# Reordering the start-up of a fused attention kernel: two queues, one product, four rows of ones

## The reference, cut to what matters

```
h = layernorm(x + causal_attention(x))            # 16 heads of 16 features
h = layernorm(h + cross_attention(h, context))
h = layernorm(h + relu(h @ w1.T + b1) @ w2.T + b2)
qp = h @ Wq + bq;  kp = ctx @ Wk + bk;  vp = ctx @ Wv + bv      # one head
w  = softmax(qp @ kp.T / 16);  y = w @ vp
g  = sigmoid(concat(qp, y) @ Wg + bg)
out = y * mask * g + h
```

## Time and profile before

| | us |
|---|---|
| three runs | 855.65, 855.28, 859.28 (median 855.65) |
| the profiled execution's own time | 855.65 |
| span of its trace | 853.8 |
| PE busy | 774.1 (91%) |
| DVE busy | 658.6 (77%) |
| POOL busy | 485.9 (57%) |
| ACT busy | 439.7 (52%) |
| start of the second stage (first instructions of SP, PE, POOL) | about 75.6 |

### The profile page before, as it was taken

How to read it: one execution, slowest core, us unless ns; L and a number is a source line. 1 busy time by engine, 2 the same in 40 slices (tenths; PEclk the granted TensorE clock), 3 DMA queues, 4 the chain that set the end, 5 groups by cost and what they waited for, 6 DMA issues and landing times.

```text
span 853.8 us, 19936 instructions
## 1 busy us (share of the span) xinstructions
PE 774.1 (91%) x7214; PEld 643.2 (75%) x7232; DVE 658.6 (77%) x1514; ACT 439.7 (52%) x921; POOL 485.9 (57%) x598
## 2 busy tenths in 40 slices
PE   6997799999999898778789999999999888999886
PEld 4766678888877676556468888888878788889875
DVE  3542768787878888667989999998888776978874
ACT  3532355565665565556555555555544543544542
POOL 1411566776777666554345666566555676657541
PEclk9999999999999999899889999999999999999988
DMA  8486889688767764336332222222200020011222
GB/s 275 137 250 197 160 125 153 130 135 140 128 112 132 120 96 89 79 85 123 76 79 55 54 54 55 53 55 54 54 2 10 2 71 8 29 56 56 83 83 77
DMA packets 105308, 79.63 MB, mean 93 GB/s; under 512 B 43261, under 2 KB 101967, under 8 KB 104947
## 3 DMA queue, kind: packets, MB, share of 16 engines
q1 hardware_dynamic: 101850, 74.17, 41.5%
q10 hardware_dynamic: 3360, 4.18, 1.5%
HBM read 27.03 MB, written 12.97 MB: 47 GB/s over the span
## 4 chain that ended last, share of the span: by engine, by line
PE 62%; DVE 17%; issue 5%; SPq 2%; ACT 2%; DMA 2%; POOL 1%; ACTq 0%; POOLq 0%; DVEq 0%
PE a_misc L88 13%; PE a_pair L88 11%; PE a_s L1009 7%; PE a_pair L796 4%; PE a_s L772 4%; PE a_pair L814 4%; PE a_pair L970 3%; PE a_s L770 3%; PE a_pair L955 3%; PE a_s L932 2%; PE a_pair L1108 2%; PE a_s L88 2%; DVE c_z L1515 1%; PE a_pair L817 1%; SPq L697 1%
## 5 line engine op out<-in xcount | busy, mean ns | idle before, releaser
L1413 DVE TENSOR_REDUCE a_nm<-a_s 128x2 f32<-128x512 f32 (+1 forms) x192 | 127.2, 678 | 56.3 <-PE a_s L772 55.6
L1924 POOL TENSOR_TENSOR c_hidden<-c_hid,c_hidden 128x256 fp32r<-128x256 f32 x128 | 96.0, 750 | 115.2 <-DVE c_hid L1653 114.8
L1174 ACT ACTIVATE a_pT<-a_pair 128x512 f32<-128x512 f32 x192 | 113.7, 597 | 86.4 <-PE a_pair L796 79.1
L1269 ACT ACTIVATE a_pT<-a_pair 77x512 f32<-77x512 f32 x128 | 76.1, 594 | 141.6 <-PE a_pair L955 137.1
L1009 PE MATMUL a_s<-c_w,c_hidden 128*128 128x256 f32 x768 | 117.4, 292 | 0.0
L88 PE MATMUL a_pair<-c_fxh,c_w 128*128 128x256 f32 x512 | 100.7, 289 | 13.9 <-DVE c_hid L1653 13.9
L1831 POOL TENSOR_SCALAR_AFFINE_SELECT a_pT<-a_pT 128x256 f32<-128x256 f32 (+1 forms) x192 | 91.6, 495 | 33.0 <-ACT a_pT L1174 32.6
L1009 PEld LDWEIGHTS a_s<-c_w,c_hidden 128*128 128x128 f32 x768 | 98.9, 190 | 0.4 <-issue 0.4
L88 PEld LDWEIGHTS a_pair<-c_fxh,c_w 128*128 128x128 f32 x512 | 79.2, 191 | 16.8 <-DVE c_hid L1653 16.7
L796 PE MATMUL a_pair<-a_sq,a_sk 98*128 98x256 bf16 (+1 forms) x512 | 76.6, 254 | 7.1 <-ACT a_pT L1174 7.0
L1653 DVE TENSOR_SCALAR c_hid<-a_pair,ff_b_col 128x256 f32<-128x256 f32 x128 | 61.3, 479 | 25.8 <-ACT c_hidden L1295 25.6
(11 more groups left out here) (258 smaller groups left out, 2143.5 us busy)
## 6 DMA issues: line engine op xcount, KB each, us to landing
a_sq<-a_parts SPq DMA_DIRECT2D x96, 128.0 KB, 4.4
a_sk<-a_parts SPq DMA_DIRECT2D x96, 128.0 KB, 4.6
a_sq<-c_parts SPq DMA_DIRECT2D x96, 128.0 KB
x<-in_xT SPq DMA_DIRECT2D x16, 256.0 KB, 6.1
res<-in_x SPq DMA_DIRECT2D x16, 256.0 KB, 5.6
out<-g_fin SPq DMA_DIRECT2D x16, 256.0 KB, 2.1
a_sk<-kc_parts SPq DMA_DIRECT2D x96, 38.5 KB
fold_rows<-x_fold ACTq DMA_DIRECT2D x1, 2496.0 KB, 9.9
```

Source lines behind the costliest of these rows:

```text
L1174: nc.scalar.activation(pT[g % NPT][:], stps[g % 2][:], ACT.Exp).then_inc(s_exp, 1)
L1269: nc.scalar.activation(pT[g % NPX][0:SC], st_ps[0:SC, :], ACT.Exp).then_inc(c_exp, 1)
L1413: nc.vector.tensor_reduce(nm[c % 2][:, QT * heads[0] + qt:QT * heads[-1] + qt + 1:QT], sps[g % 2][:].rearrange("p (h k) -> p h k", h=len(h ...
L1924: nc.gpsimd.tensor_tensor(hl(m), hid[n % NHID][:], f32(hh(m)), ALU.subtract).then_inc(c_hl, 1)
```

## The change

Five things are moved, and nothing that reaches the output changes.

1. The load of WkT goes from SP's queue, where it was first, to ACT's, where it is now first, ahead of WqT and cwk. SP's queue begins with the context.
2. PE's `square(1)` (WvT by wg2) goes from before the key loop to after it.
3. The store of the key parts (`kc_parts`) goes from SP's queue to ACT's, behind the folded keys and `part_one(1)`; on SP, the loads of sequences 2 and 3 go behind the first sequence's stacks.
4. ACT splits sequence 0 one step later in the key loop (after step 4 instead of 3), and POOL makes its low part after all six steps, not after step 4.
5. The three transfers that copied the ones at the start of the second stage are gone, and so is the memset on DVE in the first stage. Instead DVE writes the ones into each of the four stacks by a memset of 2x2048 float32, in slots 8 to 11 of causal position -2, ahead of its first maximum.

```diff
--- before.py
+++ after.py
@@ -37,7 +37,6 @@
 KS = NTERM * DH
 KX = KS + 2
 NSTK, EARLY = 4, 2
-PAIR_OF_ONES = 1.0 + 0x3F80 / 2.0 ** 23
 CB = 6
 CCH = [(c * SC, min(CB, B - c) * SC) for c in range(0, B, CB)]
 SCE = SC + 1
@@ -168,7 +167,6 @@
         @block.sync
         def _(sp):
             src = a["ctxT"].rearrange("(k p) c -> p k c", p=P)
-            sp.dma_start(raw["wkT"], lay(a["WkT"])).then_inc(w_loaded["wkT"], 16)
             for i, (c0, cn) in enumerate(CCH):
                 sp.dma_start(cf[:, :, c0:c0 + cn], src[:, :, c0:c0 + cn]).then_inc(c_loaded[i], 16)
             for n, w in (("cwv", A("ca_wv")), ("wv", a["L1_xattn_Wv"]), ("wg1", a["L1_xattn_Wg"][0:D, :]), ("swq", A("sa_wq")),
@@ -181,17 +179,15 @@
             for n, v in t.cols.items():
                 sp.dma_start(v[:], a[n + "_col"]).then_inc(small, 16)
             sp.dma_start(t.mask[:], a["maskT"]).then_inc(small, 16)
-            sp.wait_ge(s_kp3, KT * NC)
-            sp.dma_start(d.kc.rearrange("p t b x -> p (t b x)"), parts[:].rearrange("p t b k s -> p (t b k s)")).then_inc(k_stored, 16)
             sp.wait_ge(t.s_xl, EARLY)
-            for c in (2, 3):
-                sp.dma_start(t.x[c % 2][:], a["xT"][c].rearrange("(k p) s -> p k s", p=P)).then_inc(t.x_loaded[c % 2], 16)
             sp.wait_ge(t.s_p3, 1)
             for rows, term, i in stack_rows():
                 sp.dma_start(t.first_stack[0][rows].rearrange("r h s -> r (h s)"),
                              t.parts[0][:, 0, term].rearrange("p k s -> p (k s)")).then_inc(t.stacked[0], 16)
                 sp.dma_start(t.first_stack[1][rows].rearrange("r h s -> r (h s)"),
                              t.parts[0][:, 1, i].rearrange("p k s -> p (k s)")).then_inc(t.stacked[0], 16)
+            for c in (2, 3):
+                sp.dma_start(t.x[c % 2][:], a["xT"][c].rearrange("(k p) s -> p k s", p=P)).then_inc(t.x_loaded[c % 2], 16)
             sp.wait_ge(s_rowl, 1)
             sp.dma_start(d.row, f32(row[:].rearrange("o x c -> o (x c)"))).then_inc(row_stored, 16)
             sp.wait_ge(s_cbl, NC)
@@ -226,9 +222,6 @@
             pe.wait_ge(w_loaded["wkT"], 16)
             pe.wait_ge(w_loaded["wqT"], 16)
             square(0, "wkT", "wqT").then_inc(s_wkq, 1)
-            pe.wait_ge(w_loaded["wvT"], 16)
-            pe.wait_ge(w_loaded["wg2"], 16)
-            square(1, "wvT", "wg2").then_inc(s_w2, 1)
             for n in range(KT * NC):
                 ot, c = divmod(n, NC)
                 c0, cn = CCH[c]
@@ -240,6 +233,9 @@
                 mm3(nc.tensor, kps[n % 2][:, 0:cn], lambda x, kt: cwk[x][:, kt, ot * P:(ot + 1) * P],
                     lambda y, kt: (ch, cl)[y][:, kt, c0:c0 + cn], range(KT)).then_inc(s_k, 1)
 
+            pe.wait_ge(w_loaded["wvT"], 16)
+            pe.wait_ge(w_loaded["wg2"], 16)
+            square(1, "wvT", "wg2").then_inc(s_w2, 1)
             pe.wait_ge(small, 16 * (len(t.rows) + len(t.cols) + 1 + 2))
             bq, bk, bv = t.cols["bq"], t.cols["bk"], t.cols["bv"]
             for ot in range(KT):
@@ -294,7 +290,7 @@
 
         @block.scalar
         def _(act):
-            for n, w in (("wqT", a["WqT"]), ("cwk", A("ca_wk")), ("wvT", a["WvT"]), ("wg2", a["L1_xattn_Wg"][D:2 * D, :])):
+            for n, w in (("wkT", a["WkT"]), ("wqT", a["WqT"]), ("cwk", A("ca_wk")), ("wvT", a["WvT"]), ("wg2", a["L1_xattn_Wg"][D:2 * D, :])):
                 act.dma_start(raw[n], lay(w)).then_inc(w_loaded[n], 16)
             act.dma_start(bgr[:], a["L1_xattn_bg"].unsqueeze(0)).then_inc(small, 16)
             act.dma_start(bvr[:], a["L1_xattn_bv"].unsqueeze(0)).then_inc(small, 16)
@@ -327,7 +323,7 @@
                 nc.scalar.activation(parts[:, 1, c0 // SC:(c0 + cn) // SC, ot, :], byb(rest[n % 2], 0, cn), ACT.Copy).then_inc(s_kp2, 1)
                 if n in (2, 3):
                     weight_high(n - 1)
-                if n == 3:
+                if n == 4:
                     x_high(0)
             act.wait_ge(s_wkq, 1)
             nc.scalar.activation(wkq[0][:], two(fps[0]), ACT.Copy, scale=SCALE).then_inc(s_wkqh, 1)
@@ -346,6 +342,8 @@
                                      bias=colv[:, ot:ot + 1]).then_inc(s_ah, 1)
                 if n == NC:
                     part_one(1)
+            act.wait_ge(s_kp3, KT * NC)
+            act.dma_start(d.kc.rearrange("p t b x -> p (t b x)"), parts[:].rearrange("p t b k s -> p (t b k s)")).then_inc(k_stored, 16)
             act.wait_ge(s_cb, NC)
             for c, (c0, cn) in enumerate(CCH):
                 act.wait_ge(s_cbf, c + 1)
@@ -373,7 +371,6 @@
                 dve.wait_ge(s_wh, i + 1)
                 nc.vector.scalar_tensor_tensor(lo, raw[n], s, f32(hi), ALU.mult, ALU.subtract).then_inc(s_wl, 1)
 
-            nc.vector.memset(t.first_stack[1][KS:KX].bitcast(F32), PAIR_OF_ONES)
             weight_low(0)
             for c, (c0, cn) in enumerate(CCH):
                 dve.wait_ge(s_ch, c + 1)
@@ -447,18 +444,16 @@
                                         pattern=[[-1, P]], channel_multiplier=1).then_inc(const_made, 1)
             nc.gpsimd.affine_select(out=t.maskb[:], in_=t.maskb[:], compare_op=ALU.is_ge, fill=MASK, base=0,
                                     pattern=[[0, G], [-1, P]], channel_multiplier=1).then_inc(const_made, 1)
-            def x_low(c):
-                pool.wait_ge(t.s_xh, c + 1)
-                nc.gpsimd.tensor_tensor(t.xl[c][:], t.x[c][:], f32(t.xh[c][:]), ALU.subtract).then_inc(t.s_xl, 1)
-
             for n in range(KT * NC):
                 ot, c = divmod(n, NC)
                 c0, cn = CCH[c]
                 pool.wait_ge(s_kp2, n + 1)
                 nc.gpsimd.tensor_tensor(parts[:, 2, c0 // SC:(c0 + cn) // SC, ot, :], byb(rest[n % 2], 0, cn),
                                         parts[:, 1, c0 // SC:(c0 + cn) // SC, ot, :], ALU.subtract).then_inc(s_kp3, 1)
-                if n == 4:
-                    x_low(0)
+
+            def x_low(c):
+                pool.wait_ge(t.s_xh, c + 1)
+                nc.gpsimd.tensor_tensor(t.xl[c][:], t.x[c][:], f32(t.xh[c][:]), ALU.subtract).then_inc(t.s_xl, 1)
 
             def part_two(c):
                 pool.wait_ge(t.s_r1, 2 * (c + 1))
@@ -469,6 +464,7 @@
                 nc.gpsimd.tensor_tensor(t.parts[c][:, :, 2, :, :], t.rest[:].rearrange("p (w k) s -> p w k s", w=2),
                                         t.parts[c][:, :, 1, :, :], ALU.subtract).then_inc(t.s_p3, 1)
 
+            x_low(0)
             x_low(1)
             part_two(0)
             part_three(0)
@@ -482,6 +478,7 @@
 
     sb = lambda n, s, ty: placed(nc, ctx, t, "a_" + n, s, ty)
     ps = lambda n, c: ctx.enter_context(nc.psum_tensor("a_" + n, [P, c], F32))
+    PAIR_OF_ONES = 1.0 + 0x3F80 / 2.0 ** 23
     U, V, VS = 12, 8, 6
     NU = U * B
     NPT, NVP, NPX, NHID = 6, 4, 4, 3
@@ -788,7 +785,7 @@
                 kt, heads, q0 = turned_unit(u)
                 w = S - q0
                 if g == 0:
-                    pe.wait_ge(sk_ones, 16 * (NSTK - 1))
+                    pe.wait_ge(sk_ones, NSTK)
                 if u == 0:
                     pe.wait_ge(shifted[c % 2], 16 * (c // 2 + 1))
                 atleast(pe, s_exp, g - 1)
@@ -1390,8 +1387,6 @@
                 if k == 3:
                     normed(e + 3)
 
-            for v in sk[1:]:
-                act.dma_start(v[KS:KX].rearrange("r h s -> r (h s)"), sk[0][KS:KX].rearrange("r h s -> r (h s)")).then_inc(sk_ones, 16)
             for stage, n, s in order:
                 if stage == CAUSAL:
                     causal_slot(n, s)
@@ -1497,6 +1492,8 @@
                     turn_av(n - 2, 0)
                 if s in (6, 7):
                     remainder(n + 2, s - 6)
+                if n == -2 and s >= 8:
+                    nc.vector.memset(sk[s - 8][KS:KX].bitcast(F32), PAIR_OF_ONES).then_inc(sk_ones, 1)
                 if s == 8:
                     turn_back(n - 2, 0)
                 if s == 11:
```

## The result

The changed kernel takes 868.05 us (median of 4 runs, 866.52 to 870.03) against 857.46 beside it (4 runs): ratio 1.0112, 95% interval 1.0069 to 1.0155. It is slower; I had 859.5 and a range up to 863.0. A second comparison with more runs gave 1.0099 (1.0063 to 1.0136). The profiled execution took 866.2 us itself, its span is 864.4, 10.6 more than the first profile of before. How much of those 10.6 us is the change is the first thing to settle.

A forecast was written before the change was run, and what follows sets the result against it. The prediction took the kernel to be bound mostly by PE, then DVE. Its terms, -0.3 + 0.5 + 2.5 + 1.2 = +3.9 us, on 855.65 gave 859.5 us, range 855.8 to 863.0.

The forecast's parts named there:

- Part 5, the first maximum +2.5 us late: Start of second stage: four memsets of 1.765 us delay DVE's first maximum by 2.5 us, bounds 2.2 and 2.6.
- The clock after the stop, +1.2: Second stage: after PE stands 3.0 us, its clock drops to 0.50, costing 1.2 us, bounds 0 and 1.7.
- Parts 1 and 2, -0.3: First stage: reordered loads and moved square product start sequence 0's projection at 29.7, not 29.95, 0.3 us earlier.
- Rival (c): First stage gains 3.7 us, projection before 26.9, no clock drop: -0.7 in all, 854.9 us; chance 0.1.
- Part 3, +0.5: Key parts' store, issued at 46 to 50, costs 0.5 us through the value loop, bounds -1 to +3.
- the spill: Around 48 to 56: 2.9 us of moved transfers exceed the free DMA time and spill over.
- the ring: Value loop: four tiles (8 us) for stores to land; it already ran dry once, ACT idling 3.69 us.
- Part 4, nothing: First stage: splitting sequence 0 later costs nothing, as PE's projection waits for the vectors until 29.7.
- The sum: Whole kernel: the terms -0.3, +0.5, +2.5 and +1.2 add up to +3.9 us.
- the base: Whole kernel: 855.65 us, the profiled execution's own time and median of three runs, to which +3.9 was added.

The follow-up runs named there:

- e1: Changed kernel with the ones written by one first-stage memset and copied by three transfers, as before: 862.23 us (12 runs), ratio to before 1.0019.
- e2: Kernel before with only the four memsets of ones on DVE ahead of its first maximum, no transfers: 865.97 us (9 runs), ratio 1.008.
- e9: Changed kernel, unaltered, timed again beside the kernel before with more runs: 866.3 us (6 runs), ratio 1.0099.
- e3: Changed kernel with the key parts' store and the loads of sequences 2 and 3 back on SP's queue: 865.82 us (12 runs), ratio 1.0058.
- e13: Kernel before with loads reordered, square product after key loop, sequence 0 split later, folded keys' store issued at once: 858.69 us (12 runs), ratio 1.0003.
- e12: Kernel before with loads reordered, square product after the key loop and sequence 0 split later only: 857.58 us (12 runs), ratio 0.9993.
- e8: Kernel before, unaltered, profiled a second time: 860.68 us (one run).

## Why the prediction was wrong

- **Part 5, the first maximum +2.5 us late.** This is the step that failed. The mechanism was right (memsets ahead of the maximum, PE short of work, stacks behind it), the term was mis-sized: 4.1 us, since a memset takes DVE 2.14 us from start to start and not the recorded 1.765. With the clock behind it, part 5 was forecast at 3.7 us and measured at 6.5 (e1, e2). I had weighed the Trainium skill's rule against two rows of recorded durations and believed the rows; but a single memset, with DVE idle ahead of it, can't show the part that its record leaves out. The two rows' slope of 0.83 ns an element ought to have warned me: it is faster than the one element a cycle, 1.04 ns, of that rule.
- **The clock after the stop, +1.2.** It fell, and the lag grew by 1.3 between the first maximum and the stacks. The stop was 4.80 us and not 3.0. Not foreseen: at the next stop, at the stacks of sequence 2, PE worked at the lower level for 5.7 us and not 3.4, another 1.3.
- **Parts 1 and 2, -0.3.** -3.2 in the pair of traces, -2.1 against the second profile (its projection is at 28.82), -0.9 against e2's 27.62. In the ten traces that have both edits it starts between 26.6 and 27.4, so the gain was mis-sized too, but part of the 3.2 is the late start of the one profile that I predicted from. I had WqT at 8.0 and it came at 7.6; cwk at 9.9, where it was 8.9, so places in the queue gave too late a time; the first key step took 1.56 us (11.71 to 13.27) and not 2.1; the vectors ran at the full pace for which I had kept a bound only (22.57 to 26.3, 3.8 us and not 5.4). Rival (c)'s condition, a projection before 26.9, was met in the first profile (26.76) and not in e9's (27.29); its price fell short because the ones cost more.
- **Part 3, +0.5.** 1.3 in the lags (-3.19 to -1.85) and 1.5 by e3, inside the bounds -1 to +3: the spill did meet the ring. I had the store at 46 to 50; ACT issued it at 40.82.
- **Part 4, nothing.** POOL's low part became the last to arrive (0.43 us of PE waiting in the changed kernel, in 0.5 that I allowed).
- **The sum.** -3.2 + 1.3 + 4.1 + 1.3 + 1.3 = +4.8, the lag at 140 us, against +3.9. That the two are near is luck, since two large errors have opposite signs. The time missed by 8.5 us all the same, because
- **the base was wrong.** I took 855.65, which was the own time of the profile and the median of three runs; the median of 89 is 859.3. From there, the forecast's +3.9 would have been 863.2, and the measured time less that is 4.9. The range was built on bounds of my terms and had nothing in it for the clock of TensorE differing from one execution to the next by 0.02, which is 11 us here.

What stays open: why e13, 3.8 us ahead at 140 us in its profile, shows nothing in 12 timed runs. For e12 little was there to show: it is 1.2 us ahead of the first profile of before and 0.4 ahead of e8. The clock in the late part took e13's lead back in the profiles (it is level with e8 by 750 us and 1.9 ahead at the end); whether it does so as a rule was not tried.

## What to carry to other kernels

Ask of an instruction that is repeated how long it is from start to start, not how long it is recorded. Where the trace shows only single ones, take the larger of the record and a rule for the throughput: here the rule gave 4.0 us, the record 2.5, and 4.1 was measured. Put constants on an engine that is idle at that time, not ahead of the first link of the chain. And before the last few microseconds of a difference are explained, profile the old kernel twice: here its two profiles end 4.9 us apart, and the later one lost that behind 600 us, where its granted clock is the lower.

## What the runs showed of the hardware

- DVE memsets of 2048 and 1024 float32 start 2.14 and 1.07 us apart and are recorded with 1.76 and 0.91; on POOL, three of 2048 took 5.51. The part that DVE's record leaves out stands ahead of it.
- The granted clock reads 1.00 in the first 12 us of the changed kernel, where the same float32 product takes 3.75 us that takes 1.89 later. By its pace PE is at the lower level, 1.2 GHz, and the column doesn't show it.
- Around the stop of about 3 us at sequence 2's stacks the granted clock was 0.50 for 3.4 us in the first profile of before and for 6.8 in that of the changed kernel, about 1.1 of it before PE's restart.
